# A recommendation tower on one NeuronCore: quarters of a tile through every stage, written out, instead of whole tiles in a loop

## The chip, the cores and the metric

One core of one Trainium2 chip. The metric is the time of one execution in microseconds (us). The kernel before was timed in 3 runs: median 779.56 us, from 778.5 to 780.78. The profile is one further execution.

## What is computed

For each of 2048 samples, 26 embedding rows of 64 floats are fetched by index from 26 tables, which the kernel keeps stacked in one. The core of the reference:

```python
x = layer_norm(dense_t @ Wd.T, gd, bd)                      # 2048 x 128
y = layer_norm(einsum('bnd,ed->bne', sparse_t, Ws), gs, bs) # sparse_t: 26 gathered rows of 64
y = einsum('bne,pn->bep', y, Wsi)                           # 26 rows mixed into 32
y = layer_norm(y, gsi, bsi)                                 # over the 32
T = concatenate([x[:, None, :], swapaxes(y, 1, 2)], axis=1) # 33 vectors of 128
Z = einsum('bnd,bmd->bnm', T, T)                            # all inner products
z = layer_norm(Z[:, TRIL_I, TRIL_J] @ Wl.T, gl, bl) * mask  # 528 -> 512, first 384 used
h = relu(concatenate([z, r_dense_t], axis=1) @ W_top1 + b_top1)
h = relu(h @ W_top2 + b_top2)
out = h @ W_top3
```

## The kernel before, in words

The 2048 samples are 16 tiles of 128. A tile's 3328 embedding rows are 13 chunks (two blocks of 128 rows each side by side, [128, 128] floats), gathered by Pool into `rows[par]`, one of two buffers that take turns. For each chunk Pool adds `row_base` to two columns of indices (L570) and issues two indirect transfers (L574). The chunks form four `GROUPS` of 4, 4, 4 and 1, each with a semaphore `gathered`. Pool waits for nothing but the buffer's last use, two tiles ago (`rows_scaled`).

The stages of a tile, with the functions' names:

- `turn` (TensorE, L646) transposes a group's chunks, `keep_turned` (ScalarE, L941) takes them out of PSUM, `gram_product` (TensorE, L656) multiplies them by a 128x128 matrix, `square_form` (VectorE, L436) multiplies that by the rows, `row_mean_square` (L444) sums it for the variance of every row of the whole tile at once, `row_root` (ScalarE, L949) and `row_reciprocal` (L451) make 1/sigma, `scale_rows` (L458) applies it.
- `mix` (TensorE, L716) mixes the 26 features into 32, a quarter of the tile (32 samples) into one PSUM bank. `keep_high` (ScalarE, L912) and `keep_low` (VectorE, L388) split the result into two parts for `project` (TensorE, L729 and L730: two products into each of banks b and c), and `keep_y` (VectorE, L400) takes each of the two blocks out with a bias.
- `square` (ScalarE, L896), `y_mean_square` (VectorE, L410), `y_root` (ScalarE, L903), the reciprocal (L417) and `y_scale` (L424) are the second layer norm.
- `interact` (TensorE, L681) makes the inner products of a quarter with 32 small products (64 instructions), `keep_z` takes them out (two quarters on VectorE, L379, two on ScalarE, L889). SyncE then writes the tile's products to memory (`zx`) and reads them back in another layout in seven transfers (`zd`).
- `linear` (TensorE, L694, five steps into one bank), its layer norm (L966, L970, L467, L977), `turn_z` (L701), `keep_turned_z` (L983), and the top: `first_layer` (L745), `relu_1` (L919), `second_layer` (L756), `relu_2`, `third_layer` (L763), `keep_out` (L934).

Each engine runs its own program in order and meets the others at semaphores. `over_tiles` calls each engine's `tile_work` with what is due: tile t's groups after the turning, t-1's last interactions, products and linear, t-2's top. Tiles 0 to 3 and the last ones are written out, tiles 4 to 13 run as a loop of two. `turn` of tile t+1 stands in the second half of tile t's work, and `row_mean_square` waits for all four groups of the tile. Ahead of tile 0 stands the preparation of weights and of `x`.

## Time and profile before

| | |
|---|---|
| median of 3 runs | 779.56 us |
| profiled execution, its own time | 779.52 us |
| its span, first to last instruction | 777.7 us |
| busy: TensorE, VectorE, ScalarE, Pool | 582.8, 487.4, 294.0, 455.2 us |
| granted TensorE clock, mean | 0.871 |

So 1.8 us of the execution lie outside the span. Busy time is an average over stages with different limits; the clock is a share of 2.4 GHz, so 0.50 is the lower of the two levels, 1.2 GHz.

### The profile page before, as it was taken

The page shows a single profiled execution, that of the slowest core. Times are in us where ns is not written, and L with a number is a line of the kernel's source. Part 1 is how long each engine was busy: PE and PEld are TensorE (multiplying, and loading weights), DVE is VectorE, ACT ScalarE, POOL GpSimd, SP SyncE. Part 2 cuts the span into 40 slices and gives each one's busy share as a digit, 9 for nine tenths or more (in the row PEclk, how much of TensorE's full clock was granted, in tenths as well). Part 3 has the DMA queues.
Part 4 walks back from the last instruction along what each step waited for, and adds up shares of the span by engine and source line. Part 5 has one row for each costly group of instructions (what it writes and reads, how often), then busy time and mean ns, then how long its engine had stood idle before and what let it go on. Part 6 is the DMA issues. An engine that isn't in the chain of part 4 may idle for free.

```text
span 777.7 us, 18327 instructions
## 1 busy us (share of the span) xinstructions
PE 582.8 (75%) x6783; PEld 476.5 (61%) x6783; DVE 487.4 (63%) x773; ACT 294.0 (38%) x711; POOL 455.2 (59%) x628
## 2 busy tenths in 40 slices
PE   4447556869786987778778888678788887879767
PEld 3334344867675775657667676566667675758555
DVE  4628556559583958467574867458485867768810
ACT  1305533235353534243353334235353434344512
POOL 5666666666666666666666666666666666660000
PEclk9669787779899899998798899879899899999989
DMA  8200011020200202020210202121110202020110
GB/s 305 104 20 21 21 50 38 22 67 21 68 20 22 68 20 67 22 67 22 64 24 22 66 20 67 24 63 25 51 37 22 67 22 67 22 66 6 47 48 1
DMA packets 27200, 36.49 MB, mean 47 GB/s; under 512 B 8917, under 2 KB 17775, under 8 KB 26607
## 3 DMA queue, kind: packets, MB, share of 16 engines
q1 hardware_dynamic: 13808, 21.65, 7.9%
q0 software_dynamic: 13312, 13.66, 7.8%
q8 instruction: 64, 1.05, 0.5%
q14 instruction: 16, 0.13, 0.1%
HBM read 26.09 MB, written 9.18 MB: 45 GB/s over the span
## 4 chain that ended last, share of the span: by engine, by line
POOL 47%; issue 42%; PE 6%; POOLq 1%; DMA 1%; DVE 1%; ACT 1%; SPq 0%; DVEq 0%; ACTq 0%
POOL rows L574 41%; POOL ids L570 6%; PE bank_d L745 2%; PE bank_z L694 1%; PE bank_z L681 1%; POOLq L572 1%; PE bank_z L756 0%; POOLq L573 0%; PE bank_d L716 0%; DMA zx<-zs 0%; DVE y_var L410 0%; DMA rows<-in_table,ids 0%; PE bank_z L763 0%; PE bank_a L716 0%; DMA row_base<-in_row_base 0%
## 5 line engine op out<-in xcount | busy, mean ns | idle before, releaser
L574 POOL DMA_INDIRECT rows<-in_table,ids x416 | 407.0, 978 | 237.7 <-issue 198.8
L681 PE MATMUL bank_z<-r_vec 128*32 128x35 f32 x4096 | 77.6, 204 | 48.1 <-issue 47.3
L681 PEld LDWEIGHTS bank_z<-r_vec 128*32 128x32 f32 x4096 | 58.3, 112 | 71.7 <-issue 67.3
L896 ACT ACTIVATE y_sq<-y 128x512 f32<-128x512 f32 x128 | 75.3, 626 | 66.5 <-DVE y L400 55.8
L379 DVE COPY zs<-bank_z 128x280 f32<-128x280 f32 x32 | 14.4, 450 | 126.2 <-PE bank_z L681 65.9
L694 PE MATMUL bank_z<-wl,zd 128*128 128x512 f32 x160 | 83.2, 639 | 8.4 <-DMA zd<-zx 8.4
L424 DVE TENSOR_TENSOR r_vec<-y,y_r 128x512 f32<-128x512 f32 x128 | 83.3, 692 | 2.2
L912 ACT CAST mixed<-bank_d 64x512 fp32r<-64x512 f32 x64 | 37.1, 580 | 124.4 <-PE bank_d L716 66.0
L729 PE MATMUL bank_b<-mixed,proj_hi 128*128 128x512 f32 x64 | 36.5, 570 | 61.8 <-DVE mixed L388 59.9
L410 DVE TENSOR_REDUCE y_var<-y_sq 128x32 f32<-128x1024 f32 x64 | 77.4, 1210 | 0.7 <-ACT y_sq L896 0.7
L912 ACT CAST mixed<-bank_a 64x512 fp32r<-64x512 f32 x64 | 37.1, 579 | 75.5 <-PE bank_a L716 55.0
L745 PE MATMUL bank_d<-z_t,w 128*128 128x128 f32 x384 | 64.7, 312 | 0.0
L646 PE MATMUL bank_z<-ident,rows 128*128 128x128 f32 x208 | 38.6, 306 | 33.5 <-DMA rows<-in_table,ids 31.2
L646 PEld LDWEIGHTS bank_z<-ident,rows 128*128 128x128 f32 x208 | 30.2, 161 | 51.0 <-DMA rows<-in_table,ids 36.4
L388 DVE TENSOR_TENSOR mixed<-bank_a,mixed 64x512 fp32r<-64x512 f32 x64 | 44.1, 689 | 26.7 <-ACT mixed L912 22.7
L729 PEld LDWEIGHTS bank_b<-mixed,proj_hi 128*128 128x128 f32 x64 | 13.8, 215 | 75.2 <-DVE mixed L388 69.0
L716 PE MATMUL bank_d<-wsi_b,scaled 128*128 128x192 f32 (+3 forms) x256 | 58.3, 388 | 0.0
L716 PEld LDWEIGHTS bank_d<-wsi_b,scaled 128*128 128x128 f32 x256 | 55.5, 258 | 3.8
L694 PEld LDWEIGHTS bank_z<-wl,zd 128*128 128x128 f32 x160 | 44.7, 303 | 21.4 <-issue 12.5
L745 PEld LDWEIGHTS bank_d<-z_t,w 128*128 128x128 f32 x384 | 56.5, 221 | 1.5 <-ACT z_t L983 0.5
L436 DVE TENSOR_TENSOR scaled<-bank_b,rows 128x512 f32<-128x512 f32 x32 | 22.0, 687 | 54.5 <-PE bank_b L656 45.5
L570 POOL TENSOR_TENSOR ids<-ids_all,row_base 128x2 int32<-128x2 int32 x208 | 48.0, 231 | 7.3 <-DMA row_base<-in_row_base 3.1
(114 smaller groups left out, 1012.7 us busy)
## 6 DMA issues: line engine op xcount, KB each, us to landing
zx<-zs SPq DMA_DIRECT2D x16, 560.0 KB
rows<-in_table,ids POOLq DMA_INDIRECT x416
dense_t<-in_dense_t SPq DMA_DIRECT2D x1, 2048.0 KB
wl<-in_wl SPq DMA_DIRECT2D x1, 1280.0 KB
w<-in_w SPq DMA_DIRECT2D x1, 1280.0 KB
zd<-zx SPq DMA_DIRECT2D x16, 80.0 KB
wsi_b<-in_wsi_b SPq DMA_DIRECT2D x1, 1248.0 KB
zd<-zx SPq DMA_DIRECT2D x16, 70.0 KB
```

What stands on the lines that cost most here:

```text
L410: v.tensor_reduce(y_var[:, j, :], y_sq[:, j % 2, :, :].rearrange("e a (s p) -> e (a s) p", p=PROJ), AX_X, ALU.add).then_inc(y_var_done, 1)
L424: ins = v.tensor_tensor(r_vec[:, quad:quad + SPB // QUAD, :, Y0:PAD], y[:, Y_PART[j], blk, :].rearrange("e (g s p) -> e g s p", g=SPB // Q ...
L570: nc.gpsimd.tensor_tensor(ids[par][:, n:n + 2], ids_all[:, bass.ds(t * (2 * CHUNKS) + n, 2)], row_base[:, n:n + 2], ALU.add).then_inc(ids_ ...
L574: nc.gpsimd.indirect_dma_start(rows[par][:, c, D * blk:D * (blk + 1)], None, io["table"], bass.IndirectOffsetOnAxis(ap=ids[par][:, n:n + 1 ...
L646: mm = pe.transpose(bank_t[g % 2][:, n * P:(n + 1) * P], rows[par][:, c, :], ident[:])
L681: mm = pe.matmul(bank_z[PROJ * s:PROJ * (s + 1), j, n * ITEMS:(n + 1) * ITEMS], own[:, Y0:PAD], own, start=True, stop=True)
L694: mm = pe.matmul(bank_l, zd[:, :, s], wl[:, s, :], start=(s == 0), stop=(s == STEPS - 1))
L716: mm = pe.matmul(bank_m[j % 2][:, o:o + k * PROJ], scaled[:, c, :], wsi_b[:, w0:w0 + k, :], start=(n == 0), stop=(n == len(wins) - 1), ski ...
L729: pe.matmul(bank_g[blk][:], proj_hi[:], mixed[:, j % 2, blk, :], start=True, stop=False)
L745: mm = pe.matmul(bank_d[:, k * TILE:(k + 1) * TILE], w1[:, c, k * P:(k + 1) * P], z_t[:, c, :] if c < 3 else dense[c - 3], start=(c == 0), ...
L896: nc.scalar.activation(y_sq[:, j % 2, blk, :], y[:, Y_PART[j], blk, :], ACT.Square)\
L912: nc.scalar.copy(mixed[own, j % 2, blk, :], bank_m[j % 2][own, :]).then_inc(mix_hi, 1)
```

## The change

`GROUPS` become 4, 3, 3 and 3 chunks, which is what each quarter of `mix` needs. The work of the three engines goes by quarters: `w` counts 64 quarters and 8 more stages for what is left behind. Stage w takes quarter w from its turning to `keep_y`, the second layer norm and interaction of quarter w-1, and a quarter share of the linear step of the tile before and of the top of the tile before that. `row_mean_square`, `row_root` and `row_reciprocal` run four times a tile, on 6 or 8 columns. Each stage has its own PSUM bank: turning and gram share bank 0 of `bank_z`, `interact` has bank 1, `mix` bank a alone (it had a and d in turns), the projections b and c. `y` has two parts and not three. All four `keep_z` are on ScalarE. All loops but Pool's are gone; Pool and SyncE do what they did. The operations and their shapes stay, but for the splitting into groups.

```diff
-GROUPS = [range(c, min(c + 4, CHUNKS)) for c in range(0, CHUNKS, 4)]
+GROUPS = [range(0, 4), range(4, 7), range(7, 10), range(10, 13)]
+STAGES = QUARTERS + 2 * BANKS
...
-        bank_g = [bank_b, bank_c]
-        bank_m = [bank_a, bank_d]
+        bank_y = [bank_b, bank_c]
+        bank_m = bank_a
+        bank_t = bank_g = bank_z[:, 0, :]
+        bank_i = bank_z[:, 1, :]
...
+            for w in range(STAGES):
+                tile, q = divmod(w, BANKS)
+                new, old = w < QUARTERS, 1 <= w <= QUARTERS
+                if old:
+                    y_mean_square(w - 1)
+                if new:
+                    square_form(w)
+                    row_mean_square(w)
+                if old:
+                    y_reciprocal(w - 1)
+                    y_scale(w - 1, 0)
+                if new:
+                    row_reciprocal(w)
+                    scale_rows(w)
+                if old:
+                    y_scale(w - 1, 1)
...
+                if new:
+                    keep_low(w, 0)
+                    keep_low(w, 1)
+                    keep_y(w, 0)
+                    keep_y(w, 1)
...
+            def turn(k):
+                t, q = divmod(k, BANKS)
+                pe.wait_ge(gathered[t % 2][q], (t // 2 + 1) * (32 * len(GROUPS[q])))
+                if k:
+                    pe.wait_ge(quad_done, k)
...
+                if new:
+                    turn(w)
+                if top and q == 0:
+                    turn_z(tile - 2)
+                if top and q == 2:
+                    second_layer(tile - 2)
+                if top and q == 3:
+                    third_layer(tile - 2)
+                if new:
+                    gram_product(w)
...
+                if 1 <= tile <= TILES and q == 3:
+                    linear(tile - 1, range(2, STEPS))
+                if new:
+                    mix(w)
+                if old:
+                    interact(w - 1)
+                if new:
+                    project(w)
...
+            for w in range(STAGES):
+                if old:
+                    square(w - 1, 0)
+                    square(w - 1, 1)
+                if new:
+                    keep_turned(w)
...
+                if old:
+                    y_root(w - 1)
+                if new:
+                    row_root(w)
...
+                if new:
+                    keep_high(w, 0)
+                    keep_high(w, 1)
...
+                if old:
+                    keep_z(w - 1)
```

On TensorE before, the second half of a tile written out (tile 3) reads so:

```order
L716 MATMUL bank_d<-wsi_b,scaled 128x160
L646 MATMUL bank_z<-ident,rows 128x128 x4
L729 MATMUL bank_b<-mixed,proj_hi 128x512
L730 MATMUL bank_b<-mixed,proj_lo 128x512
L729 MATMUL bank_c<-mixed,proj_hi 128x512
L730 MATMUL bank_c<-mixed,proj_lo 128x512
L646 MATMUL bank_z<-ident,rows 128x128 x4
L694 MATMUL bank_z<-wl,zd 128x512
```

The last quarter of a tile on TensorE in the changed kernel (L617 is the turning, L708 the third layer, L623 the gram product, L670 linear, L634 the mixing, L657 the interaction, L643 and L644 the projection):

```order
L617 MATMUL bank_z<-ident,rows 128x128 x3
L708 MATMUL bank_z<-h,w 1x128 x2
L623 MATMUL bank_z<-gram,rows_t 128x128 x3
L670 MATMUL bank_z<-wl,zd 128x512 x3
L634 MATMUL bank_a<-wsi_b,scaled 128x96
L634 MATMUL bank_a<-wsi_b,scaled 128x192 x2
L634 MATMUL bank_a<-wsi_b,scaled 128x160
L657 MATMUL bank_z<-r_vec 32x35 x32
L643 MATMUL bank_b<-mixed,proj_hi 128x512
L644 MATMUL bank_b<-mixed,proj_lo 128x512
```

Before, groups of the next tile were turned in one place and mixed half a tile later, and the mixing of one quarter stood ahead of the projection of the one before. Now a quarter's turning, gram product, mixing and projection follow one another in the same stage.

On VectorE before, a tile begins with all four groups and one sum over them:

```order
L436 TENSOR_TENSOR scaled<-bank_b,rows 128x512
L436 TENSOR_TENSOR scaled<-bank_c,rows 128x512
L436 TENSOR_TENSOR scaled<-bank_b,rows 128x512
L436 TENSOR_TENSOR scaled<-bank_c,rows 128x128
L444 TENSOR_REDUCE row_var<-scaled 128x26
L451 RECIPROCAL row_r<-row_std 128x26
L458 TENSOR_TENSOR scaled<-rows,row_r 128x512
```

One quarter on VectorE in the changed kernel (L382 `square_form`, L391 its sum, L442 and L450 the second layer norm of the quarter before, L400 and L407 the first one of this quarter, L417 `keep_low`, L425 `keep_y`):

```order
L382 TENSOR_TENSOR scaled<-bank_z,rows 128x384
L391 TENSOR_REDUCE row_var<-scaled 128x6
L442 RECIPROCAL y_r<-y_std 128x32
L450 TENSOR_TENSOR r_vec<-y,y_r 128x16x32
L400 RECIPROCAL row_r<-row_std 128x6
L407 TENSOR_TENSOR scaled<-rows,row_r 128x384
L450 TENSOR_TENSOR r_vec<-y,y_r 128x16x32
L462 RECIPROCAL l_r<-l_std 128x1
L417 TENSOR_TENSOR mixed<-bank_a,mixed 64x512 x2
L425 TENSOR_TENSOR y<-bank_b,y_bias 128x512
L425 TENSOR_TENSOR y<-bank_c,y_bias 128x512
```

The first layer norm of a quarter now stands between the `y_mean_square` and the `y_scale` of the quarter before, and `keep_low` and `keep_y` of the same quarter behind them.

## Rows read from the trace of the kernel before

**Rows 1.** The page: chain that ended last, by line, shares of the span.

```profile
POOL rows L574 41%; POOL ids L570 6%; PE bank_d L745 2%; PE bank_z L694 1%; PE bank_z L681 1%; POOLq L572 1%; PE bank_z L756 0%; POOLq L573 0%; PE bank_d L716 0%; DMA zx<-zs 0%; DVE y_var L410 0%; DMA rows<-in_table,ids 0%; PE bank_z L763 0%; PE bank_a L716 0%; DMA row_base<-in_row_base 0%
```

**Rows 2.** Groups by line, Pool: count, busy us, mean ns, idle before.

```profile
L574 POOL DMA_INDIRECT rows<-in_table,ids x416 | 407.0, 978 | 237.7 <-issue 198.8 <-POOL ids L570 38.9
L570 POOL TENSOR_TENSOR ids<-ids_all,row_base 128x2 int32<-128x2 int32 x208 | 48.0, 231 | 7.3 <-DMA row_base<-in_row_base 3.1
```

**Rows 3.** The chain that ended last: start us, us, what.

```profile
4.66 1.09 POOL rows L574
...
699.50 2.34 DMA rows<-in_table,ids
...
728.36 0.03 issue
...
749.56 2.94 DMA zx<-zs
...
756.57 6.72 PE bank_z L694 x10
```

**Rows 4.** Groups by line and shape, VectorE.

```profile
L424 DVE TENSOR_TENSOR r_vec<-y,y_r 128x512 f32<-128x512 f32 x128 | 83.3, 692 | 2.2
L410 DVE TENSOR_REDUCE y_var<-y_sq 128x32 f32<-128x1024 f32 x64 | 77.4, 1210 | 0.7 <-ACT y_sq L896 0.7
L388 DVE TENSOR_TENSOR mixed<-bank_a,mixed 64x512 fp32r<-64x512 f32 x64 | 44.1, 689 | 26.7 <-ACT mixed L912 22.7 <-issue 2.3
L400 DVE TENSOR_TENSOR y<-bank_c,y_bias 128x512 f32<-128x512 f32 x64 | 43.7, 683 | 3.6 <-PE bank_c L730 3.3 <-issue 0.2
L458 DVE TENSOR_TENSOR scaled<-rows,row_r 128x512 f32<-128x512 f32 x48 | 31.6, 687 | 0.5
L444 DVE TENSOR_REDUCE row_var<-scaled 128x26 f32<-128x1664 f32 x16 | 30.2, 1886 | 0.6
L436 DVE TENSOR_TENSOR scaled<-bank_b,rows 128x512 f32<-128x512 f32 x32 | 22.0, 687 | 54.5 <-PE bank_b L656 45.5 <-issue 9.0
L417 DVE RECIPROCAL y_r<-y_std 128x32 f32<-128x32 f32 x64 | 21.9, 342 | 0.5
...
L436 DVE TENSOR_TENSOR scaled<-bank_c,rows 128x128 f32<-128x128 f32 x16 | 4.5, 280 | 0.0
```

**Rows 5.** The same, ScalarE.

```profile
L896 ACT ACTIVATE y_sq<-y 128x512 f32<-128x512 f32 x128 | 75.3, 626 | 66.5 <-DVE y L400 55.8 <-issue 10.7
...
L912 ACT CAST mixed<-bank_a 64x512 fp32r<-64x512 f32 x64 | 37.1, 579 | 75.5 <-PE bank_a L716 55.0 <-issue 19.3
```

**Rows 6.** Timeline of TensorE: start us, us, line, count.

```profile
32.63 1.97 PE L646 MATMUL bank_z<-ident,rows 128*128 128x128 f32 x8 [2.24 <-DVE x_t L332]
...
505.89 2.40 PE L716 MATMUL bank_a<-wsi_b,scaled 128*128 128x160 f32 x8
...
712.49 1.28 PE L716 MATMUL bank_a<-wsi_b,scaled 128*128 128x160 f32 x8
...
719.98 0.77 PE L681 MATMUL bank_z<-r_vec 128*32 128x35 f32 x64
...
727.44 0.40 PE L729 MATMUL bank_c<-mixed,proj_hi 128*128 128x512 f32 x1
...
727.67 0.39 PE L730 MATMUL bank_c<-mixed,proj_lo 128*128 128x512 f32 x1
...
731.21 3.60 PE L694 MATMUL bank_z<-wl,zd 128*128 128x512 f32 x8
...
734.65 1.95 PE L756 MATMUL bank_z<-h,w 128*128 128x128 f32 x16
```

**Rows 7.** Stretches: length, busy us and count by engine, granted clock, DMA.

```profile
442.00:486.00 44.00, 36.53 (x429) 29.94 (x428) 31.40 (x49) 17.92 (x43) 29.27 (x41) 0.92 0.15 41
486.00:530.00 44.00, 32.76 (x403) 28.17 (x402) 24.86 (x40) 15.87 (x39) 28.68 (x40) 0.81 0.16 42
...
503.00:509.00 6.00, 5.94 (x46) 5.85 (x46) 1.65 (x3) 0.58 (x1) 4.09 (x5) 0.55 0.10 23
```

More of the change, by code:

```diff
@@ L86, in block_rows, with group_of @@
     return PLACES[k][0], PROJ - PLACES[k][1]
+def group_of(c):
+    return next(g for g, chunks in enumerate(GROUPS) if c in chunks)
 WINDOWS, WIN_COLS = chunk_windows()
@@ L331, in finish_x @@
                 dve.wait_ge(pe_prep, 8 + j)
[L332 removed]
+                step(v.tensor_scalar(x_t[:, j * BANK:(j + 1) * BANK], bank_x[j % 2][:], col["gd"], col["bd"],
                                      ALU.mult, ALU.add), "end" if j == 3 else f"x{j}")
@@ new lines, in mix @@
+            def mix(k):
+                q = k % BANKS
+                pe.wait_ge(rows_scaled, k + 1)
+                if k:
+                    pe.wait_ge(mix_lo, 2 * k)
+                wins = [w for w in WINDOWS if w[3] == q]
+                for n, (c, s0, num, _, w0) in enumerate(wins):
+                    o = (s0 - q * SPB) * PROJ
+                    mm = pe.matmul(bank_m[:, o:o + num * PROJ], scaled[:, c, :], wsi_b[:, w0:w0 + num, :],
+                                   start=(n == 0), stop=(n == len(wins) - 1), skip_group_check=True)
+                mm.then_inc(mix_done, 1)
@@ new lines, in linear @@
+            def linear(t, steps):
+                if steps[0] == 0:
+                    pe.wait_ge(z_moved, Z_MOVES * (t + 1))
+                    pe.wait_ge(sumx_placed, t + 1)
+                    if t:
+                        pe.wait_ge(z_kept, t)
+                    else:
+                        pe.wait_ge(wl_centred, 1)
+                for s in steps:
+                    mm = pe.matmul(bank_l, zd[:, :, s], wl[:, s, :], start=(s == 0), stop=(s == STEPS - 1))
+                if steps[-1] == STEPS - 1:
+                    mm.then_inc(l_done, 1)
@@ L776, in tile_work @@
-                if top:
-                    first_layer(0)
-                if inter:
-                    interact(0)
-                    interact(1)
-                if top:
-                    first_layer(1)
-                if load and not inter:
-                    fold(range(0, 1))
-                    fold(range(1, 3))
-                if load:
-                    mix(0)
-                if top:
-                    first_layer(2)
-                if load and not inter:
-                    add_up_x(0)
@@ L792, in tile_work @@
-                if top:
-                    first_layer(3)
-                if load:
-                    project(0)
-                if inter:
-                    interact(2)
-                if load:
-                    mix(1)
-                if load and not inter:
-                    fold(range(3, STEPS))
-                if load:
-                    mix(2)
-                if inter:
-                    interact(3)
-                if load:
-                    project(1)
-                    mix(3)
@@ L825, in tile_work @@
-                if more:
-                    turn(t + 1, 1 - par, 2)
-                if load and not inter:
-                    add_up_x(3)
-                if inter:
-                    linear(range(3, STEPS))
-                if more:
-                    turn(t + 1, 1 - par, 3)
-                if inter and not top:
-                    fold_bl()
-                if top:
-                    second_layer()
-                if more:
-                    gram_product(t + 1, 0)
-                    gram_product(t + 1, 1)
@@ new lines, in third_layer @@
+            def third_layer(t):
+                pe.wait_ge(h2_kept, t + 1)
+                for c in range(2):
+                    mm = pe.matmul(bank_w[0:1, 0:TILE], w3[:, c:c + 1], h2[:, c, :], start=(c == 0), stop=(c == 1))
+                mm.then_inc(out_done, 1)
+            for w in range(STAGES):
+                tile, q = divmod(w, BANKS)
+                new, old = w < QUARTERS, 1 <= w <= QUARTERS
+                top = 2 <= tile <= TILES + 1
+                if new:
[8 more added lines that the diff above has]
+                    gram_product(w)
+                if w < 4:
+                    add_up_x(w)
+                if w == 1:
+                    fold()
+                if w == 4:
+                    fold_bl()
+                if top and q == 0:
+                    first_layer(tile - 2, range(0, 2))
+                if top and q == 1:
+                    first_layer(tile - 2, range(2, 4))
+                if 1 <= tile <= TILES and q == 2:
+                    linear(tile - 1, range(0, 2))
+                if 1 <= tile <= TILES and q == 3:
[6 more added lines that the diff above has]
+                    project(w)
```

689 lines of the change are left out of this document (260 added, 429 removed).

## The prediction

> **What bounds the kernel now.** I read the page's chain first, because busy shares of four engines between 38% and 75% name no bound. Its shares by line [rows 1] put two fifths on Pool's indirect transfers, and no line of another engine has more than 2%. The chain itself [rows 3] runs through Pool from the first transfer at 4.66 us to the last, issued at 699.50. Between the two there are 415 steps, so one transfer takes (699.50 - 4.66) / 415 = 1.674 us. The Pool groups [rows 2] agree: 407.0 busy and 237.7 idle, of which nearly all is "issue", that is, Pool waits for nobody. A tile of 26 transfers costs Pool 43.5 us, a quarter of three chunks 10.05, one of four 13.4. Whatever the other engines do, the last rows land at 699.50 + 2.34 = 701.84.
>
> The second half of the answer is the tail. From 701.84 to the span's end at 777.7 are 75.9 us, in which the last tile goes through all its stages, with the first layer norm of all 13 chunks ahead of the first mixing and the last transfer of products to memory starting only at 749.56 [rows 3]. From there to the end 28.1 us go into that transfer, its seven reads, linear (6.72 at a clock that had fallen during the wait) and the top.
>
> **What the change does, part by part.** Pool and SyncE keep their instructions, so the 701.84 stays if Pool is still never held up. The tail shrinks, because only the last quarter is left when the last rows land. The danger is the stage's own chain. Within a stage every engine is in order, TensorE can't turn quarter w+1 before it has projected quarter w, and this can't start before VectorE's `keep_low` of w. One bank for each step leaves nothing to run ahead. So a stage has a latency, and 64 of them must keep up with Pool.
>
> I add that latency up from the end of the projection of quarter w-1 to the same point of w, at the full clock. VectorE [rows 4]: second `keep_y` 0.68, `y_mean_square` 1.21, `square_form` on 384 columns 0.55 (between 0.280 for 128 and 0.687 for 512, in proportion), `row_mean_square` on 384 elements 0.53 (1.886 at 1664 and 1.210 at 1024 give 1.056 ns an element), `y_reciprocal` 0.34, first `y_scale` 0.69, `row_reciprocal` on 6 columns 0.2 (between nothing and the 0.342 of 32 columns), `scale_rows` 0.55 (shape as `square_form`, 0.687 at 512), second `keep_low` 0.69. Together 5.44. ScalarE [rows 5]: second `square` 0.63 and two `keep_high` 1.16, together 1.79. TensorE [rows 6]: `mix` 1.28, and the second block's projection, from 727.44 to 727.67 + 0.39 = 0.62, together 1.90. The handoffs are about a dozen of 0.03 to 0.04 [rows 3], 0.5. The sum is 9.6. Beside it lie, unpaid: the copy of the turned quarter and the gram product, under `y_mean_square` (the copy at most 0.6 and six instructions of the product at most 6/8 of the 1.28 of `mix`; I let 0.2 stick out); `row_root`, under `y_reciprocal`; `interact` of the quarter before, 0.77 [rows 6], under the first `keep_high` and `keep_low` (0.58 + 0.69). That gives 9.8 a stage.
>
> Per tile come on top: the fourth chunk of the first quarter, 0.14 in each of three VectorE steps, 0.5; the second layer, 1.95 for its 16 instructions [rows 6], which now stands between turning and gram product of the third quarter, where about 1.4 of it is hidden by `keep_y`, `square` and the copy, 0.6; three steps of linear, 2.7 from 3.60 for four steps [rows 6], which stand in the last quarter between gram product and `mix`, where VectorE needs 2.9 (`square_form` to `scale_rows`), 0.2 for safety. A tile is then 4 x 9.8 + 1.3 = 40.5 against Pool's 43.5. The chain fits, with 3.0 us a tile to spare. The extra work of splitting the row statistics (three more reductions, roots and reciprocals a tile) is in the 9.8. The two copies of products moved from VectorE to ScalarE stand behind `keep_high` and off this chain.
>
> The first turning was at 32.63 [rows 6], since the preparation ahead of it stays. The fold of Wl, the sums of x, their scalings and the top's weights now sit in stages 0 to 5; I take 8 us for them, my own choice and from no row. Quarter 0 had landed 13 us earlier than stage 0 begins, so the stages start about 20 us behind Pool, and 3.0 a tile take that back in seven tiles. Pool itself would be held up only if `scale_rows` of tile t-2 were later than Pool's end of tile t-1, a whole tile (43.5) after its last rows; a lag of 20 doesn't reach it.
>
> **The end.** With the lag gone, stage 62 begins when its rows land, 10.05 before 701.84, takes 9.8 + 0.6 and ends at 702.2; stage 63, with linear's 0.2, ends its projection at 712.2. Behind it: `keep_y` 0.68, `square` 0.63, `y_mean_square` 1.21, the root and the reciprocal 0.34 each, two `y_scale` 1.38, `interact` 0.77, the copy about 0.45, handoffs 0.3, so the products leave at 718.3 instead of 749.56. The rest is what it was, 28.1: span 746.4, execution 748.2 with the 1.8 outside the span. I add 3 us, for a stage or two at the end in which the clock is low (a `mix` took 2.40 instead of 1.28 [rows 6]) or `interact` is not fed fast enough. **Forecast 751 us.** The profiled execution (779.52) and the median (779.56) are the same, so no correction.
>
> **Where a rule speaks against it.** The granted clock in the loop was 0.92 in one tile's stretch and 0.81 in the next, and it stayed at 0.55 through six us in which TensorE was busy 5.94 [rows 7]. What stood ahead of such stretches were waits of three us and more. In the new chain TensorE's longest idle piece is about 1.4 us (from turning to gram product), and it works some 7 of 9.8 us. The Trainium skill, in "TensorE: Matmul & The Clock Gate", section "A second HAM failure mode: psum-queue depth-cycling", says that short idles between groups of products, as a kernel cycles through PSUM banks, are enough to make the clock swing between its two levels. By that rule this kernel would be the third case below; the rows don't show whether idles this short do it.
>
> **The rivals.** First, **clock as before.** At 1.2 GHz throughout, a stage gains on `mix` 1.12 [rows 6], on the projection about 0.55 and on the gram product about 0.7 in the same proportion, 9.5 a tile, with 1.7 for the second layer and 2.4 for linear: 54 instead of 40.5. If the clock is 0.87 over all, 26% of the time is at the low level, and a tile takes 1 / (0.26/54 + 0.74/40.5) = 43.3, just Pool's rate. The early lag is then never taken back, and the end is 32.6 + 8 + 16 x 43.3 + 34.2 (tail behind the last projection) + 1.8 = 769. The same comes out if at full clock each `interact` sticks out by 0.7. For it: nothing in the change removes the clock's falls by itself. Against it: the long waits behind which it fell, for all four groups and for the transfers, are gone.
>
> Second, the other side, **the stage chain becomes the bound.** At the 0.81 of the bad stretch [rows 7], 38% of the time is low and a tile takes 44.7; the end is 40.6 + 715 + 36 = 792. It decides from a tile of 43.9 on (40.6 + 702.9 + 36 = 779.5), which is 1.0 a stage more than I summed. For it speaks that the margin is 7% of a sum of thirteen steps, with no slack between them. Against it, that low clock makes TensorE's idles shorter and so works against itself.
>
> Third, **the change doesn't shorten the tail as I say**, since the top of tile 14 and the stages' fixed order are queued ahead of tile 15's last steps. They would have to fill more than the waits for the products' transfer, and first layer halves and 1.95 of second layer don't; I give 3 to 5 us to it, inside the forecast's range.
>
> **How the numbers follow.** Pool stays the bound and the lag is taken back: 0.66, 744 to 758, likeliest 751; the lower end is no extra 3 and 4 less in the tail. In between, as in the first rival: 0.14, 758 to 777. Within 0.3% (about 2.3 us, what a measurement can tell from no change): 0.03. The stage chain bounds and it is slower: 0.17, 782 to 810. The range 744 to 780 leaves out that last case and a little below. Faster 0.80, same 0.03, slower 0.17.
>
> **What would show it.** Right: Pool's groups unchanged with the last transfer issued at about 699.5; TensorE's turning waiting for rows in the later tiles; a distance of about 10.9 from one stage to the next late in the run and 9.8 to 10.5 early; products leaving near 718; a granted clock of 0.93 or more. Wrong: Pool's chain broken by waits for `scaled` rows, a stage distance above 11 in the second half with turning never waiting for a transfer, `mix` near 2.4 in most stages, `interact` with gaps that hold up the projection.

## The result, and the profile after

The changed kernel took 756.64 us, the median of 3 runs (754.51 to 757.04), against 779.56. The ratio is 0.9698 (0.9662 to 0.9734): 3.0% faster. The forecast was 751, its range 744 to 780. A ratio here and below leaves out executions over 1.5% slower than the fastest of the same kernel; a median holds all.

The profiled execution has a span of 754.8 us, 8.4 more than the 746.4 that the prediction summed. The page of the changed kernel gives first the busy time of each engine, then TensorE's granted clock in 40 slices, then the chain that ended last, by engine and by line.

```profile
PE 568.3 (75%) x6783; PEld 439.8 (58%) x6783; DVE 501.8 (66%) x837; ACT 333.4 (44%) x791; POOL 460.1 (61%) x628
...
PEclk9779879999999999999999799999999899997999
...
POOL 47%; issue 42%; PE 5%; DMA 2%; POOLq 1%; DVE 1%; ACT 1%; SPq 0%; DVEq 0%; ACTq 0%
POOL rows L549 40%; POOL ids L545 7%; PE bank_d L690 1%; PE bank_z L670 1%; DMA zx<-zs 1%; POOLq L547 1%; PE bank_a L634 1%; PE bank_z L701 1%; POOLq L548 0%; DMA rows<-in_table,ids 0%; PE bank_z L623 0%; DMA row_base<-in_row_base 0%; DVE mixed L417 0%; SPq L520 0%; ACT mixed L818 0%
```

The chain is the same as in [rows 1]: Pool's transfers and adds, then a tail. The mean clock was 0.932 instead of 0.871. Next the groups by line of the same kernel: Pool, and TensorE's small interaction products (busy us, mean ns, idle before).

```profile
L549 POOL DMA_INDIRECT rows<-in_table,ids x416 | 407.8, 980 | 237.5 <-POOL ids L545 165.8 <-issue 71.6
L545 POOL TENSOR_TENSOR ids<-ids_all,row_base 128x2 int32<-128x2 int32 x208 | 52.2, 251 | 7.4 <-DMA row_base<-in_row_base 3.1
...
L657 PE MATMUL bank_z<-r_vec 128*32 128x35 f32 x4096 | 55.9, 202 | 0.8 <-DVE r_vec L450 0.5
```

Pool waits for nobody, as before, but against [rows 2] its adds took 251 ns on average instead of 231, 4.2 us in all, and its transfers 0.8 more. The timeline of Pool ends with its last transfer, issued at 704.16 (699.50 in [rows 3]); issuing it took 1.04.

```profile
702.90 0.96 POOL L549 DMA_INDIRECT rows<-in_table,ids  x1 [0.81 <-POOL ids L545]
704.16 1.04 POOL L549 DMA_INDIRECT rows<-in_table,ids  x1 [0.30 <-issue]
```

The timeline of TensorE's turnings (L617) shows both halves of the run. Early on a tile's first turning follows the one before at 40.3 or 41.0 us and waits for no transfer; later it waits for rows.

```profile
167.26 0.60 PE L617 MATMUL bank_z<-ident,rows 128*128 128x128 f32 x4
...
207.56 0.60 PE L617 MATMUL bank_z<-ident,rows 128*128 128x128 f32 x4
...
248.57 0.60 PE L617 MATMUL bank_z<-ident,rows 128*128 128x128 f32 x4
...
589.70 1.11 PE L617 MATMUL bank_z<-ident,rows 128*128 128x128 f32 x4 [3.06 <-DMA rows<-in_table,ids]
...
688.00 0.90 PE L617 MATMUL bank_z<-ident,rows 128*128 128x128 f32 x3 [1.85 <-DMA rows<-in_table,ids]
698.58 0.49 PE L617 MATMUL bank_z<-ident,rows 128*128 128x128 f32 x3
708.49 0.49 PE L617 MATMUL bank_z<-ident,rows 128*128 128x128 f32 x3
```

So the stages start behind Pool, catch up at 40.3 to 41.0 us a tile, and from the turning at 371.97 on, the first that waits for rows, run at Pool's rate. The last wait is that of stage 61. The chain that ended last runs through it, over the transfer issued at 684.58, and on to the last quarter (start us, us, what):

```profile
684.58 3.37 DMA rows<-in_table,ids
...
708.69 0.70 DVE y L425
...
709.95 0.47 ACT rows_t L801
710.46 0.95 PE bank_z L623 x6
711.44 0.57 DVE scaled L382
...
713.70 0.57 DVE scaled L407
714.31 1.43 PE bank_a L634 x8
715.76 0.59 ACT mixed L818
716.38 0.70 DVE mixed L417
...
724.71 4.61 DMA zx<-zs
```

Nearly every step hands over to another engine: this is the stage's latency that the prediction summed. The products leave at 724.71, where it was 749.56.

### The profile page after: what moved, and what is told of

Same layout as the page of the kernel before. It is cut to its first block, busy times and chain, and to the rows that moved or that the text cites. A ratio compares the mean times of both kernels' runs of the same rounds, so it can differ in the third digit from the quotient of the medians.

```text
span 754.8 us, 18142 instructions
## 1 busy us (share of the span) xinstructions
PE 568.3 (75%) x6783; PEld 439.8 (58%) x6783; DVE 501.8 (66%) x837; ACT 333.4 (44%) x791; POOL 460.1 (61%) x628
## 4 chain that ended last, share of the span: by engine, by line
POOL 47%; issue 42%; PE 5%; DMA 2%; POOLq 1%; DVE 1%; ACT 1%; SPq 0%; DVEq 0%; ACTq 0%
POOL rows L549 40%; POOL ids L545 7%; PE bank_d L690 1%; PE bank_z L670 1%; DMA zx<-zs 1%; POOLq L547 1%; PE bank_a L634 1%; PE bank_z L701 1%; POOLq L548 0%; DMA rows<-in_table,ids 0%; PE bank_z L623 0%; DMA row_base<-in_row_base 0%; DVE mixed L417 0%; SPq L520 0%; ACT mixed L818 0%
## 5 line engine op out<-in xcount | busy, mean ns | idle before, releaser
L417 DVE TENSOR_TENSOR mixed<-bank_a,mixed 64x512 fp32r<-64x512 f32 x128 | 88.1, 688 | 90.5 <-ACT mixed L818 87.0
L818 ACT CAST mixed<-bank_a 64x512 fp32r<-64x512 f32 x128 | 74.3, 581 | 132.9 <-PE bank_a L634 131.3
L634 PE MATMUL bank_a<-wsi_b,scaled 128*128 128x192 f32 (+3 forms) x512 | 89.6, 319 | 44.7 <-DVE scaled L407 44.7
L634 PEld LDWEIGHTS bank_a<-wsi_b,scaled 128*128 128x128 f32 x512 | 77.7, 194 | 75.6 <-DVE scaled L407 75.0
L623 PE MATMUL bank_z<-gram,rows_t 128*128 128x128 f32 x416 | 74.7, 328 | 50.0 <-ACT rows_t L801 49.9
L623 PEld LDWEIGHTS bank_z<-gram,rows_t 128*128 128x128 f32 x416 | 62.5, 227 | 63.9 <-ACT rows_t L801 63.9
L450 DVE TENSOR_TENSOR r_vec<-y,y_r 128x512 f32<-128x512 f32 x128 | 88.2, 690 | 2.2
L670 PE MATMUL bank_z<-wl,zd 128*128 128x512 f32 x160 | 77.6, 615 | 3.2 <-DMA zd<-zx 3.2
L382 DVE TENSOR_TENSOR scaled<-bank_z,rows 128x512 f32<-128x512 f32 (+1 forms) x64 | 37.8, 591 | 47.2 <-PE bank_z L623 43.8
L643 PE MATMUL bank_b<-mixed,proj_hi 128*128 128x512 f32 x64 | 32.9, 514 | 40.5 <-DVE mixed L417 40.5
L809 ACT ACTIVATE row_std<-row_var,eps 128x8 f32<-128x8 f32 (+1 forms) x64 | 19.2, 300 | 94.3 <-DVE row_var L391 94.3
L657 PE MATMUL bank_z<-r_vec 128*32 128x35 f32 x4096 | 55.9, 202 | 0.8 <-DVE r_vec L450 0.5
L670 PEld LDWEIGHTS bank_z<-wl,zd 128*128 128x128 f32 x160 | 45.2, 301 | 16.2 <-DMA zd<-zx 3.4
L617 PE MATMUL bank_z<-ident,rows 128*128 128x128 f32 x208 | 37.3, 296 | 21.4 <-DMA rows<-in_table,ids 19.0
L657 PEld LDWEIGHTS bank_z<-r_vec 128*32 128x32 f32 x4096 | 46.6, 111 | 10.7 <-issue 4.3
L425 DVE TENSOR_TENSOR y<-bank_b,y_bias 128x512 f32<-128x512 f32 x64 | 44.3, 692 | 7.9 <-PE bank_b L644 1.8
```

The lines of the kernel that those rows point to most:

```text
L417: v.tensor_tensor(mixed[other, k % 2, blk, :], bank_m[own, :], mixed[own, k % 2, blk, :].bitcast(F32), ALU.subtract).then_inc(mix_lo, 1)
L450: ins = v.tensor_tensor(r_vec[:, quad:quad + SPB // QUAD, :, Y0:PAD], y[:, k % 2, blk, :].rearrange("e (g s p) -> e g s p", g=SPB // QUAD, ...
L623: mm = pe.matmul(bank_g[:, n * P:(n + 1) * P], rows_t[:, c, :], gram[:], start=True, stop=True)
L634: mm = pe.matmul(bank_m[:, o:o + num * PROJ], scaled[:, c, :], wsi_b[:, w0:w0 + num, :], start=(n == 0), stop=(n == len(wins) - 1), skip_g ...
L657: mm = pe.matmul(bank_i[PROJ * s:PROJ * (s + 1), n * ITEMS:(n + 1) * ITEMS], own[:, Y0:PAD], own, start=True, stop=True)
L670: mm = pe.matmul(bank_l, zd[:, :, s], wl[:, s, :], start=(s == 0), stop=(s == STEPS - 1))
```

## The experiments

They ran on three chips, on which the kernel before itself took 796.3, 781.4 and 789.3 us (medians). So only ratios and runs of one chip are compared, and every ratio is against the kernel before on the same chip.

### First chip: loops, the wait for a whole tile, a longer stage

**1. The kernel before without its loops.** All engines but Pool written out, the order as it was.

```diff
-            with eng.Fori(2, TILES // 2 - 1) as i:
-                body(i * 2, 0, True, True, True, True)
-                body(i * 2 + 1, 1, True, True, True, True)
+            if loop:
+                with eng.Fori(2, TILES // 2 - 1) as i:
+                    body(i * 2, 0, True, True, True, True)
+                    body(i * 2 + 1, 1, True, True, True, True)
+            else:
+                for t in range(4, TILES - 2):
+                    body(t, t % 2, True, True, True, True)
...
-            over_tiles(pool, gather)
+            over_tiles(pool, gather, loop=True)
```

> The kernel before with the loop of TensorE, VectorE, ScalarE written out (Pool keeps its loop), the order of work untouched. My theory: Pool sets the time up to the last rows and the tail was already written out, so 779.6 us within 0.3% (777 to 782). Rival: writing out is what brought part of the 23 us; then 757 to 775.

It took 782.78 us, ratio 0.9849 (0.9787 to 0.9911). "No change" missed: on this chip writing out gave 1.5%. But its profiled span was 779.9, and the products left at 751.15, 50.4 us after the last transfer was issued; in [rows 3], from the first result's kernel before, it is 749.56 and 50.1. The tail is the old one.

**2. The changed kernel, but a tile's first quarter waits for all four groups.** This is meant to take back only the use of quarters as they land.

```diff
-                pe.wait_ge(gathered[t % 2][q], (t // 2 + 1) * (32 * len(GROUPS[q])))
+                for g in range(BANKS if q == 0 else 0):
+                    pe.wait_ge(gathered[t % 2][g], (t // 2 + 1) * (32 * len(GROUPS[g])))
```

> The changed kernel, but the first quarter of a tile is turned only when all four quarters' rows have landed. My theory: the gain is that the last tile is three quarters done when its last rows land. Without that, the last tile starts at the last landing, about 708, takes one tile of the chain, 40.5, and the tail of 36 behind it: 784 us (780 to 790), no better than before. Rival: the gain comes from the order, the banks or the writing out; then it stays at 757 to 765.

It took 822.88 us, ratio 1.0301 (1.0239 to 1.0362). 784 was expected where the kernel before takes 779.6, so the sign is right and the size larger. Its groups by line say why:

```profile
L545 POOL TENSOR_TENSOR ids<-ids_all,row_base 128x2 int32<-128x2 int32 x208 | 49.0, 235 | 46.9 <-DVE scaled L407 39.7 <-DMA row_base<-in_row_base 3.1
...
L658 PE MATMUL bank_z<-r_vec 128*32 128x35 f32 x4096 | 79.2, 204 | 44.5 <-issue 43.1 <-DVE r_vec L450 0.5
```

With the stages a whole tile behind Pool, Pool waits 39.7 us for buffers to be scaled, so the edit delays the last rows too. And the interaction products had 43.1 us of gaps in which TensorE waited for nothing that the profile shows; in the changed kernel's first profile there were 0.8.

**3 and 4. A longer stage.** One extra product of 128 columns on VectorE ahead of `square_form` in each stage (+0.28 us by the 0.280 of [rows 4]), and, in another run, two of 512 (+1.38).

```diff
+                    v.tensor_tensor(spare[:, 0:128], ones[:], ones[:], ALU.mult)
```

```diff
+                    for part in range(2):
+                        v.tensor_tensor(spare[:, part, :], x_t[:, 0:BANK], x_t[:, 0:BANK], ALU.mult)
```

> The changed kernel with one more VectorE product of 128x128 in each quarter, ahead of square_form, about 0.29 us on the stage's chain, 1.2 us a tile. My theory: a tile of the chain goes from 40.5 to 41.7, still under Pool's 43.8, so the loss is only the one or two stages at the end: 757 to 759 us. Rival, the chain bounds already: 64 x 0.29 = 18.6 us more, 775.

> The same with two products of 128x512, about 1.3 us in each stage, 5.2 us a tile. My theory: a tile of the chain is now 45.7, above Pool's 43.8, so the chain sets the time: 33 + 9 + 16 x 45.7 + 37 = 810 us (800 to 820), above the kernel before. Rival, that stages overlap enough to hide VectorE work: 757 to 770.

The small one gave 783 to 818 us (median 802.21), too scattered for a ratio, and even its lowest is above both 757 to 759 and the rival's 775. The large one gave 861.08, ratio 1.0792 (1.0739 to 1.0846), much more than 810. Its turnings of a tile's first quarter:

```profile
429.37 0.60 PE L620 MATMUL bank_z<-ident,rows 128*128 128x128 f32 x4
...
477.19 0.60 PE L620 MATMUL bank_z<-ident,rows 128*128 128x128 f32 x4
```

That is 47.8 us a tile; the two tiles after it took 51.1 and 51.5. Over the whole run, with the 40.6 ahead and the 34.2 behind of the prediction, the span of 860.9 gives (860.9 - 74.8) / 16 = 49.1. The expected 40.3 + 4 x 1.38 = 45.8 and the interaction gaps, 53.7 us in all or 3.4 a tile, together make 49.2. That this fits so well is in part luck, because the extra products don't lie on the chain in full. In the changed kernel VectorE waits about 0.7 us a stage for the gram product ahead of `square_form`, just where they were put:

```profile
DVE scaled L382 <- PE bank_z L623: 43.8, 40, 4.3
```

In the large run only 3.8 of this wait are left. What grew instead is VectorE's idle time ahead of `keep_y`, from 7.9 to 80.8 us, mostly for the projection, which stands behind the interaction. So the gaps may cost more than their own length; how the 50 us by which the expectation missed divide was not tested. The gaps can be seen in the timeline of the small run, where 64 interaction products end only just before the projection, which starts at once:

```profile
209.33 0.69 PE L659 MATMUL bank_z<-r_vec 128*32 128x35 f32 x54
210.41 0.28 PE L659 MATMUL bank_z<-r_vec 128*32 128x35 f32 x4 [0.40 <-issue]
211.19 0.27 PE L659 MATMUL bank_z<-r_vec 128*32 128x35 f32 x5 [0.50 <-issue]
211.92 0.22 PE L659 MATMUL bank_z<-r_vec 128*32 128x35 f32 x1 [0.46 <-issue]
212.06 0.50 PE L645 MATMUL bank_b<-mixed,proj_hi 128*128 128x512 f32 x1
```

This is "`interact` sticks out", which the prediction had priced inside its first rival. Whether it came from the edits or from the chip was open: none of these kernels was the changed one itself.

### Second chip: the changed kernel again, and Pool's time

**5. The changed kernel again.**

> The changed kernel once more, as the anchor for this call's chip, because on the chip of the last four runs the kernel before took 796 and not 780, and the interactions of every experiment there had 34 to 56 us of gaps with the releaser issue, where the changed kernel's profile has 0.8. Theory A, the gaps depend on the chip or the moment: here too they can appear, and the changed kernel then takes 765 to 785. Theory B, they depend on the program: this one has none anywhere, and the ratio to the kernel before stays at 0.97.

755.49 us, ratio 0.9664 (0.9621 to 0.9707); interaction idle 0.8 us. The first result stands, and Theory B looked right here; the third chip refutes it.

**6 and 7. One add a tile instead of thirteen,** in the changed kernel and in the kernel before. The same edit in both (n counts a tile's 26 columns):

```diff
-                    if blk == 0:
-                        nc.gpsimd.tensor_tensor(ids[par][:, n:n + 2], ids_all[:, bass.ds(t * (2 * CHUNKS) + n, 2)],
-                                                row_base[:, n:n + 2], ALU.add).then_inc(ids_ready, 1)
-                        pool.wait_ge(ids_ready, t * CHUNKS + c + 1)
+                    if n == 0:
+                        nc.gpsimd.tensor_tensor(ids[par][:], ids_all[:, bass.ds(t * (2 * CHUNKS), 2 * CHUNKS)],
+                                                row_base[:], ALU.add).then_inc(ids_ready, 1)
+                        pool.wait_ge(ids_ready, t + 1)
```

> The changed kernel, but Pool adds the row bases once for all 26 columns of a tile and not 13 times for two. Without the add (0.20) and the idle behind it (0.81 in place of 0.30) a chunk costs Pool 2.5 instead of 3.24, a tile about 33.6 instead of 43.6. My theory: then the stage chain of 40.4 a tile bounds: 33 + 9 + 16 x 40.4 + 37 = 725 us, and up to 45 more if the interactions have gaps. Rival, the chain has no slack as it is (its stages wait for each other whatever Pool does): 757. Second rival, stages shorten as rows are always there: 690.

> The kernel before with the same single add per tile. Pool no longer bounds it either; what shows is how long its tile is by itself. TensorE worked 33 to 36 of 44 us a tile there with two waits of 3 us, so I expect 38 to 41 a tile and 50 + 16 x 39.5 + 60 = 740 us (720 to 760). If the order by quarters is as good or better once Pool is out of the way, it lies above the changed kernel with one add; if the order before had more overlap, below.

The changed kernel took 740.99 us, ratio 0.9486 (0.9456 to 0.9515). The kernel before took **657.34**, ratio 0.8419 (0.8391 to 0.8446), far from the 740 expected and 11% less than the changed kernel with the same edit. It beats both kernels of this case. The groups of Pool, first of the changed kernel with one add:

```profile
L549 POOL DMA_INDIRECT rows<-in_table,ids x416 | 405.6, 975 | 135.1 <-issue 122.0 <-POOL ids L545 13.1
L545 POOL TENSOR_TENSOR ids<-ids_all,row_base 128x26 int32<-128x26 int32 x16 | 7.1, 444 | 99.4 <-DVE scaled L407 96.3 <-DMA row_base<-in_row_base 3.1
```

then of the kernel before with one add:

```profile
L574 POOL DMA_INDIRECT rows<-in_table,ids x416 | 414.8, 997 | 135.1 <-issue 121.4 <-POOL ids L570 13.1 <-DVE scaled L458 0.6
L570 POOL TENSOR_TENSOR ids<-ids_all,row_base 128x26 int32<-128x26 int32 x16 | 4.5, 279 | 6.0 <-DMA row_base<-in_row_base 3.0 <-DVE scaled L458 2.8
```

The edit takes 140 us out of Pool in the kernel before, from 700.0 busy and idle to 560.4: twelve adds a tile, and behind each a pause of 0.81 instead of 0.30. In the changed order Pool then waits 96.3 us for the stages, which have become the bound. In the order before it waits 3.4, so Pool still nearly sets the pace: (414.8 + 135.1 + 4.5 + 6.0) / 16 = 35.0 a tile. The timelines of TensorE show both rates, here the turnings of the changed kernel with one add:

```profile
168.40 0.60 PE L617 MATMUL bank_z<-ident,rows 128*128 128x128 f32 x4
...
208.70 0.60 PE L617 MATMUL bank_z<-ident,rows 128*128 128x128 f32 x4
...
249.00 0.60 PE L617 MATMUL bank_z<-ident,rows 128*128 128x128 f32 x4
259.64 0.49 PE L617 MATMUL bank_z<-ident,rows 128*128 128x128 f32 x3
271.49 0.49 PE L617 MATMUL bank_z<-ident,rows 128*128 128x128 f32 x3
```

and here the first `mix` of a tile in the kernel before with one add:

```profile
553.51 1.38 PE L716 MATMUL bank_a<-wsi_b,scaled 128*128 128x160 f32 x8
...
588.04 1.28 PE L716 MATMUL bank_a<-wsi_b,scaled 128*128 128x160 f32 x8
```

40.3 us a tile against 34.5. Not every tile is like these: from tile 1 to tile 15 the mean is 41.1 in the changed kernel, where four tiles took 42.3, and 36.0 in the kernel before, where five took 38 to 40. The 42.3 make 8 of the 16 us by which the expected 725 was short; the first three tiles took 5 more than expected. The windows of the changed kernel with one add show what a tile of 42.3 contains (length, busy by engine, then the clock): one stage of 11.90 us ran at 0.71, with TensorE busy 9.87 of it, behind a stretch at 1.00.

```profile
208.70:249.00 40.30, 31.43 (x417) 24.41 (x416) 29.79 (x50) 19.72 (x46) 25.62 (x28) 1.00 0.18 45
...
259.60:271.50 11.90, 9.87 (x107) 8.79 (x106) 7.35 (x13) 5.25 (x13) 8.99 (x10) 0.71 0.36 102
```

**8. Pool alone.** Only the gathers are left: the other engines' work is taken out, Pool waits for no buffer, and the output is zeros.

> Only Pool's 416 gathers with their adds; no other engine works but for a memset and the store of zeros, so all the computation is left out. Tells what of Pool's 1.674 us a transfer is its own. Theory: its undisturbed chunk is 3.24, so the last transfer goes out at 4.7 + 208 x 3.24 = 678 us, and the other engines' work costs it 22 us before and 28 after, which is where the changed kernel's 6 us went. Rival: Pool's pace is its own and varies by execution; then about 700.

One run, 690.83 us. Pool's groups:

```profile
L297 POOL DMA_INDIRECT rows<-in_table,ids x416 | 396.2, 953 | 237.4 <-POOL ids L293 165.6 <-issue 71.8
L293 POOL TENSOR_TENSOR ids<-ids_all,row_base 128x2 int32<-128x2 int32 x208 | 42.4, 204 | 7.4 <-DMA row_base<-in_row_base 3.2
```

The last transfer was issued at 683.00; 678 was expected, and 699.50 in the kernel before. The idle time is what it was to 0.3 us, but the busy time is 438.6 us, where it was 455.0 in the kernel before and 460.0 in the changed one. So the work of the other engines costs Pool 16 us and 21 us (22 and 28 were expected): the mean of a transfer is 953 or 980 ns and that of an add 204 or 251 ns. "Whatever the other engines do" was wrong.

The traces also show where the time goes. Most of Pool's instructions last the same in all three kernels: the median of an add is 0.20 us, that of a transfer 0.95 or 0.96. Alone, not one add took more than 0.23 us and not one transfer more than 1.10; in the changed kernel 28 adds and 35 transfers did, and they hold 20 us more than the medians. In the kernel before it was 16 and 31, with 15.6 us. Of these 63 long ones 61 overlap in time with a `y_scale` or a `scale_rows` of VectorE, two products that read both inputs from SBUF; of the others one in six does. In the kernel before it is 45 of 47. No run took these products out alone, so that they are the cause is likely and not tested.

### Third chip: is it the edit or the chip?

Runs 3 and 2 again (as runs 9 and 10), with the changed kernel (run 11) beside them.

> The run with one small VectorE product more in each stage, again, beside the unchanged kernel. Without gaps inside the interactions the chain of a tile is 40.3 + 1.2 = 41.5, under Pool's 43.7: 757 to 760 us, at most 4 above the changed kernel of this call. With such gaps (34 us or more of them, as on the first chip) a tile passes Pool's time and it takes 775 or more. If it takes 775 without gaps, the stage chain bounded already and my theory of slack falls.

> The run in which a tile is turned only when all its rows have landed, again. Without gaps in the interactions: last rows about 708, the last tile's four stages 40.3 behind them, then 36: 784 to 788 us. Pool isn't held up, since a tile's last scaling lies 37 us behind its landing. If the gain had another source than the last tile's early start, it stays near 757.

> The changed kernel unchanged, the anchor of this call. 752 to 760 if its interactions have no gaps (under 2 us); if the gaps go with the chip and this is such a chip, 34 us of them or more and 765 to 785.

| | median, us | ratio | interaction gaps ("issue"), us |
|---|---|---|---|
| changed kernel (run 11) | 781.40 | 0.9915 (0.9853 to 0.9976) | 29.3 |
| one small product more in a stage (run 9) | 779.42 | 0.9889 (0.9820 to 0.9957) | 33.8 |
| first quarter waits for the tile (run 10) | 801.98 | 1.0273 (1.0139 to 1.0406) | 27.4 |

The group of the changed kernel, the same program as in the first result, on this chip:

```profile
L657 PE MATMUL bank_z<-r_vec 128*32 128x35 f32 x4096 | 72.1, 203 | 29.7 <-issue 29.3
```

So the gaps need no edit: one program had 0.8 us of idle there in two sessions and 29.7 in a third, and gained 3.0%, 3.4% and 0.9%. In its profile on this chip Pool is as quick as on the others, yet the products leave 14 us later than in the first result:

```profile
702.77 0.94 POOL L549 DMA_INDIRECT rows<-in_table,ids  x1 [0.30 <-issue]
...
738.60 4.91 DMA zx<-zs
```

Here no turning waited for rows at all. From tile 2 to tile 15 a tile took 43.2 us on average, about Pool's own rate, so the early lag was never taken back, and the stages, not Pool, set the end. This is the prediction's first rival, with gaps instead of a low clock.

The small product can't be told from no change on the same chip, where 64 x 0.28 = 18 us, or 2.3%, would show. That isn't slack against Pool, which was used up here. The product falls for the most part into VectorE's idle time ahead of `square_form`, which is 32.1 us in the profile of run 11 and 20.4 in that of run 9.

The wait for the whole tile costs 1.0273 / 0.9915 = 1.036, or 28 us (by the medians of the runs behind the two ratios, 801.98 and 778.84, it is 23). But contrary to the expectation Pool was held up, 15.8 us, and its last transfer went out 16.5 us later than in the changed kernel:

```profile
719.23 0.94 POOL L549 DMA_INDIRECT rows<-in_table,ids  x1 [0.30 <-issue]
...
770.77 2.71 DMA zx<-zs
```

So about half of the 32 us by which the products leave later is Pool's delay. The other half is the longer way behind the last transfer.

### A shorter stage that wasn't

**12. The changed kernel with one add, and a different order in the stage.** On TensorE the turning of quarter w+1 stands between `mix` and `interact` of w. On VectorE the first layer norm of a quarter stands ahead of the second one of the quarter before. On ScalarE (not shown) the copy of the turned quarter follows `keep_high`, and `row_root` stands ahead of `y_root`.

```diff
-                if new:
-                    turn(w)
+                if w == 0:
+                    turn(0)
...
                 if new:
                     mix(w)
+                if w + 1 < QUARTERS:
+                    turn(w + 1)
                 if old:
                     interact(w - 1)
```

```diff
-                if old:
-                    y_mean_square(w - 1)
                 if new:
                     square_form(w)
                     row_mean_square(w)
-                if old:
-                    y_reciprocal(w - 1)
-                    y_scale(w - 1, 0)
-                if new:
                     row_reciprocal(w)
                     scale_rows(w)
                 if old:
+                    y_mean_square(w - 1)
+                    y_reciprocal(w - 1)
+                    y_scale(w - 1, 0)
                     y_scale(w - 1, 1)
```

> The changed kernel with one add per tile on Pool and with another order inside a stage: the next quarter is turned between mix and interact and copied behind keep_high, and VectorE does square_form to scale_rows of the new quarter before y_mean_square to y_scale of the old one. Nothing is done less. My theory: the 40.3 of a tile is the length of one chain and not an engine's load; with square, y_mean_square, y_reciprocal and y_scale (about 3.2 us) beside mix and off the chain, a stage takes VectorE's 7.6 us of work and about 1 of waits, a tile 36: 42 + 16 x 36 + 37 = 655 us (645 to 675) against 741 with the one add alone. Rival, load: VectorE or TensorE can't go below 40 a tile: 735 to 741.

1206.87 us, ratio 1.541 (1.5242 to 1.5578), where 645 to 675 was expected. The stages did get shorter: the three from 455.88 to 483.19 took 27.3 us, where the same three took 29.7 in run 6 (179.04 to 208.70). But once a tile everything but Pool stands still. Its timeline of VectorE, then of Pool:

```profile
414.14 1.41 DVE L417 TENSOR_TENSOR mixed<-bank_a,mixed 64x512 fp32r<-64x512 f32 x2
439.94 0.69 DVE L425 TENSOR_TENSOR y<-bank_b,y_bias 128x512 f32<-128x512 f32 x1 [24.39 <-remote]
```

```profile
411.26 0.24 POOL L542 TENSOR_TENSOR ids<-ids_all,row_base 128x26 int32<-128x26 int32 x1 [39.00 <-DVE scaled L407]
...
443.87 0.94 POOL L546 DMA_INDIRECT rows<-in_table,ids  x1 [0.30 <-issue]
```

TensorE's records put the projection of that quarter at 418.25 to 420.4, and yet VectorE's `keep_y` and ScalarE's copy of the interactions come 16 to 20 us later, near the end of Pool's burst of 26 transfers, released by nothing that the trace names. Then Pool waits 39 us on average for the stages, and so they take turns, 71 us a tile. In run 6 the same burst lay beside the stages and stopped nothing. No packet of the instruction queues is in the trace between 416 and 456, so nothing shows that the engines went on because code had landed. What holds the two engines back is not settled, and no run was made that tells it.

## Why the prediction was right, point by point

**The bound.** Right for the first result and its repeat: Pool is still the chain, 40% and 7% by line, and waits for nobody. That makes the gain one of the tail alone. It doesn't hold on the third chip, where the stages with their gaps set the end. Run 6 shows the other face: with Pool quicker the stages bound, 41.1 a tile on average, and run 7 shows that the order before could do 36.0. The change traded throughput, which was not needed at Pool's 43.5, for a shorter way from the last rows to the end, which was.

**"The last rows land at 701.84 whatever the other engines do."** This is the mis-sized term. The last transfer was issued at 704.16 and not at 699.50, 4.7 us later, and the busy times of adds and transfers are 5.0 longer in all. Run 8 shows the coupling itself, 16 us of it already in the kernel before, in single instructions that stand beside VectorE's two products from SBUF. I took the 1.674 a transfer as Pool's own; but Pool's groups sum to 683.4 us alone, 1.643 a transfer, and to 700.0, 1.683, in the kernel before, so 0.04 of it, times 416, depends on what the others do.

**The stage's sum, 9.8, and 40.5 a tile.** Right: 40.3 or 41.0 in the early tiles of the changed kernel, 40.3 in most tiles of run 6. In stage 63 the distance from the start of one projection to that of the next was 717.12 - 707.20 = 9.92. From `keep_y` to `square_form` it took 711.44 - 708.69 = 2.75; I had 0.68 + 0.63 + 1.21 + 0.2 = 2.72. But the path there ran through the copy of the turned quarter and the gram product, not through `y_mean_square`.

**The lag of 20 us, taken back in seven tiles.** Right in kind and about right in size: up to tile 7, turned at 329.89, no turning waits for rows after the start, and tile 8's, at 371.97, is the first that does. The margin was stated a little wrong: 43.9 a tile is 3.4 over 40.5, so 0.85 a stage and not 1.0.

**The end.** By my sum stage 61's rows would have landed at 701.84 - 2 x 10.05 = 681.7 and the projection of stage 63 would have ended 30.5 later. The trace has 688.0 and 30.6. Of the 6.3, 5.0 are Pool (the same transfer, twelve ahead of the last, was issued at 684.58, and at 679.55 in the kernel before) and 1.0 is its landing, 3.37 instead of 2.34. Behind it I had 6.1 to the products' leaving, and it took from 718.58 to 724.71, 6.1. From there to the span's end I left the old 28.1; it took 30.1, since the transfer of products took 4.61 instead of 2.94 (5.02 in run 5, 3.45 in run 7; no row says why). So 8.4 = 6.3 from the rows + 0.1 + 2.0. The 3 us that I had added for other reasons, a low clock or unfed products at the end, covered part of it by luck, and 751 became 756.6.

**Where the gain comes from.** From the way behind the last transfer. In the profiles it is, in us:

| | last transfer issued | products leave | distance |
|---|---|---|---|
| kernel before | 699.50 | 749.56 | 50.1 |
| written out, old order (run 1) | 700.75 | 751.15 | 50.4 |
| changed kernel, first result | 704.16 | 724.71 | 20.6 |
| changed kernel again (run 5) | 702.66 | 723.18 | 20.5 |
| changed kernel, third chip (run 11) | 702.77 | 738.60 | 35.8 |
| first quarter waits for the tile (run 2) | 742.67 | 792.98 | 50.3 |
| the same, third chip (run 10) | 719.23 | 770.77 | 51.5 |

Writing out alone leaves the distance as it was, and the wait for the whole tile brings all of it back. The wait does more than that, since it also holds Pool up (39.7 and 15.8 us), so the 28 us it costs on the third chip are not the price of the quarters alone. On the first chip writing out gave 1.5%; on the others its share wasn't measured.

**The clock.** The first rival had "clock as before". (The passage on the rule points to "the third case below"; what it describes is this first rival.) The granted clock rose to 0.932. From 45 us on, TensorE's timeline has 25 idle stretches of two us and more in the kernel before, up to 7.6, and five in the changed one, up to 3.2. The Trainium skill, "TensorE: Matmul & The Clock Gate", section "A second HAM failure mode: psum-queue depth-cycling", speaks of short idles between groups as enough to make the clock swing. Such idles, up to 1.5 us, stand ahead of the gram products here (49.9 us in all in the changed kernel), and in run 6 a stretch of 40.3 us ran at 1.00 all the same. But now and then a stage fell, in run 6 to 0.71, and took 11.85 us instead of 9.84. So idles this short did not hold the clock down for long; whether they set off the falls that there were is not shown.

**The rival that did come, elsewhere.** I had written that 769 results "if at full clock each `interact` sticks out by 0.7". Run 11's profiled execution, with 29.3 us of gaps or 0.46 an `interact`, took 772.0, with a lag that was never taken back. So that rival was real, and on that chip the change gained 0.9%, not 3%; that would be 773 against 779.56, inside the range but in the case that I gave 0.14. The forecast was right for sessions in which the products are fed, and that this was such a session was luck: no term of the stage's sum foresaw it.

**The other side.** The chain as the bound, from 43.9 a tile on: run 4, at 49.1, is slower than before, as the price said. Run 3 and its repeat were expected at 41.5 a tile. Their profiles have 43.8 and 44.2 on average from tile 2 to tile 15, right at the border, and the repeat's ratio of 0.9889 is no loss.

## What to carry to other kernels

When one engine's queue sets the end, what a reordering of the others can win is the way from its last item to the end, and what it may spend for that is the difference of the two rates; both can be read before anything is changed. Then look at the bounding queue first: thirteen small dependent adds a tile where one would do, a quarter of a microsecond each, cost the kernel before 16% with the pauses behind them, and the order that looked slower was the better one once they were gone. A bounding engine's own durations are not a constant: they were read beside the work of the others, and their sum moved by 1 to 5% when that work changed. And an extra instruction tells a stage's slack only if it stands on the chain and not in a wait.

## What the runs showed of the hardware that was not expected

- Pool's add of two columns took 204 ns on average alone, 231 in the kernel before and 251 in the changed one; its indirect transfers 953, 978 and 980. With one add a tile in the kernel before, transfers took 997. The medians hardly move (0.20 and 0.95 or 0.96 us). The difference is in 47 and 63 long ones, of which 45 and 61 overlap with a VectorE product of two SBUF inputs; alone there was none.
- Long runs of small products (64 of 35 columns) are fed without gaps in some sessions, 0.77 us for the 64, and in others pause 0.4 to 0.5 us after every four or five. The same program had 0.8, 0.8 and 29.7 us of idle there. The kernels with loops and without both show the pauses (47.3 in the kernel before, 58.9 in run 1, which is written out), so loops aren't the cause. Nor is it the chip alone: the 47.3 are from the profile that goes with the first result, whose changed kernel had 0.8. What is stays open.
- Another order in a stage stopped two engines once a tile, for 25 to 29 us on average and at most 34, beside a burst of indirect transfers that stopped nothing in the order without it.
